# One subtile in two groups of four, in place of one in three, fetched row by row by the sync engine of a two-layer graph network

## What is computed

```python
h = relu(layernorm(x)); z = h @ W                       # per node
e = leaky_relu(el[src] + er[dst]); a = exp(e - emax[dst])
x = x + segment_sum(z[src] * a, dst) / segment_sum(a, dst) + bias
h = relu(layernorm(x)); s, v = h @ W_up                  # per node
w0..w3 = split(silu(silu(edge_f @ A1 + b1) @ A2 + b2) @ A3)
msg = [s[src]*y_s*w0, (v[src].y_v)*w3, s[src]*y_v*w1, v[src]*y_s*w2]
x = x + segment_sum(msg, dst) / 10 @ W_out
```

## Time and profile before

| | us |
|---|---|
| median of 3 runs (4036.51 to 4043.6) | 4041.5 |
| the profiled execution, its own time | 4049.47 |
| its span, first to last instruction | 4047.6 |
| POOL busy | 2961.1 (73%) |
| PE busy | 3048.9 (75%) |
| DVE busy | 1948.5 (48%) |
| ACT busy | 1119.0 (28%) |

### The profile page before, as it was taken

How to read it: one execution, slowest core, us unless ns; L and a number is a source line. 1 busy time by engine, 2 the same in 40 slices (tenths; PEclk the granted TensorE clock), 3 DMA queues, 4 the chain that set the end, 5 groups by cost and what they waited for, 6 DMA issues and landing times.

```text
span 4047.6 us, 71477 instructions
## 1 busy us (share of the span) xinstructions
PE 3048.9 (75%) x15640; PEld 2582.1 (64%) x15641; DVE 1948.5 (48%) x4563; ACT 1119.0 (28%) x1869; POOL 2961.1 (73%) x3121
## 2 busy tenths in 40 slices
PE   2566666666667656766659989888899898899898
PEld 2556665566667555665647767666677676676676
DVE  7434434333433433434345555555555555555554
ACT  2334434333433434333331111111111111111111
POOL 1777777777777777777747777777777777777775
PEclk9666666666655665666669888888988989988888
DMA  3434343443434343444422222222222222222221
GB/s 107 119 108 119 111 121 109 124 114 108 119 109 118 112 121 104 124 113 114 118 52 59 59 62 61 60 61 60 59 60 61 61 60 61 60 60 61 60 62 49
DMA packets 208656, 352.07 MB, mean 87 GB/s; under 512 B 99631, under 2 KB 129638, under 8 KB 208326
## 3 DMA queue, kind: packets, MB, share of 16 engines
q0 software_dynamic: 99328, 216.34, 21.3%
q1 hardware_dynamic: 108548, 130.56, 10.4%
q10 hardware_dynamic: 450, 2.44, 0.2%
HBM read 338.22 MB, written 10.85 MB: 86 GB/s over the span
## 4 chain that ended last, share of the span: by engine, by line
POOL 66%; issue 24%; DVE 2%; DMA 2%; PE 2%; POOLq 1%; DVEq 1%; SPq 1%; ACT 1%; ACTq 0%
POOL rows L534 66%; DMA rows<-z_tab,idx 1%; DMA rows<-up_tab,idx 1%; POOLq L280 1%; PE pair L1175 0%; SPq L333 0%; ACT L633 0%; POOLq L281 0%; DVE share L1036 0%; PE pair L1307 0%; DMA win_dram<-share 0%; DVE share L1128 0%; PE pair L1264 0%; DVEq L965 0%; PE pair L1270 0%
## 5 line engine op out<-in xcount | busy, mean ns | idle before, releaser
L534 POOL DMA_INDIRECT rows<-z_tab,idx x1552 | 1477.2, 952 | 554.6 <-issue 546.1
L534 POOL DMA_INDIRECT rows<-up_tab,idx x1552 | 1468.0, 946 | 510.3 <-issue 505.4
L1211 PE MATMUL pair<-acc 128*128 x3168 | 572.1, 327 | 443.3 <-ACT acc L621 441.0
L1211 PEld LDWEIGHTS pair<-acc 128*128 128x128 f32 x3168 | 555.3, 272 | 490.4 <-issue 490.4
L1307 PE MATMUL pair<-share 128*128 128x144 f32 x3136 | 833.8, 354 | 0.0
L1305 PEld LDWEIGHTS pair<-share 128*128 128x128 f32 x3136 | 577.1, 217 | 395.6 <-DVE share L1131 220.4
L1243 PE MATMUL pair<-share,acc 128*128 128x136 f32 x3136 | 676.6, 400 | 0.3
L1305 PE MATMUL pair<-share 128*128 128x48 f32 x3136 | 573.1, 268 | 101.3 <-DVE share L1131 101.1
L1243 PEld LDWEIGHTS pair<-share,acc 128*128 128x128 f32 x3136 | 639.2, 299 | 0.5 <-issue 0.4
L1128 DVE TENSOR_TENSOR share<-rows,pair 128x384 f32<-128x384 f32 x784 | 396.6, 547 | 412.7 <-DMA rows<-up_tab,idx 397.6
L1307 PEld LDWEIGHTS pair<-share 128*128 128x128 f32 x3136 | 544.7, 217 | 0.0
(11 more groups left out here) (172 smaller groups left out, 1890.2 us busy)
## 6 DMA issues: line engine op xcount, KB each, us to landing
acc<-dst_tab SPq DMA_DIRECT2D x198, 512.0 KB
lent<-z_tab SPq DMA_DIRECT2D x2060, 0.6 KB
lent<-up_tab SPq DMA_DIRECT2D x2060, 0.5 KB
rows<-z_tab,idx POOLq DMA_INDIRECT x1552
rows<-up_tab,idx POOLq DMA_INDIRECT x1552
ef_sb<-in_edge_f SPq DMA_DIRECT2D x198, 32.0 KB
z_tab<-rows SPq DMA_DIRECT2D x7, 504.0 KB, 3.2
y_sb<-in_edge_y SPq DMA_DIRECT2D x198, 16.0 KB
```

Source lines behind the costliest of these rows:

```text
L534: pool.indirect_dma_start(out=rows[:, s, t, 0:width], out_offset=None, in_=table, in_offset=bass.IndirectOffsetOnAxis(ap=indices[:, t:t + ...
L1211: mm = t.matmul(bank[6 + h][:, i * 16:i * 16 + 16], hotT[:, h, i * P:(i + 1) * P], er_flat[:, bass.ds(at, 1), :].rearrange("p a f -> p (a ...
```

## The change

`PER` becomes 2, so that a round is two groups; SP fetches one subtile in 64 in place of one in 96. `PARTS` becomes eight parts of 16 rows, in place of eight of 12 and four of 8. There are 24 rounds in a stage in place of 16, with one group left over in both. The table of the offsets (`lent_dram`) grows from 17 to 25 rows.

```diff
-PER = 3
+PER = 2
 LENT = GI // PER
-PARTS = (12,) * 8 + (8,) * 4
+PARTS = (16,) * 8
```

## The result

The kernel before took 4041.5 us (4036.51 to 4044.52, 5 runs), the changed one **4072.7 us** (4070.77 to 4090.51, 5 runs). The ratio is 1.0095, 95% interval 1.0068 to 1.0121: slower by about 31 us. The forecast was 4045 with a range of 4025 to 4080. The time lies in the range, but it is not "within 0.2%", which I had called likeliest.

The account below looks back on a forecast made before the run. The prediction took POOL's gathers to bound the kernel, with SP's store-to-store loop about as long in stage 1 after the change. Stage 1 +14 and stage 2 -10 gave +4 on 4041.5, so 4045 us, range 4025 to 4080.

Parts of the forecast that it names:

- within 0.2%: Whole kernel: time not told from no change, the forecast's own range of 4033 to 4050 us; chance 0.42.
- POOL as the bound, 1.251 us for each gather: Both stages: POOL waits for nobody, so each gather spared is worth 1.251 us while nothing else is as slow.
- Stage 2, -10: Stage 2: 8 gathers fewer save 10.0 us; SP's 389 us of added rows fit in its 610 us of waits.
- rival 4: Stage 2: SP fills up, at 0.6 us for a row in place of 0.38; above 4060 us, chance 0.03.
- The step with 16 rows: SP's plain step in stage 1 grows from 5.70 us with 12 rows to 7.22 with 16.
- Leg A: Stage 1, from one block's store to the next over a round's end: grows from 38.62 to 43.2 us.
- Leg B: Stage 1, store to next store inside a round: 36.2 us, with PE fast on the second of two tiles.
- rival 2: Stage 1: PE slow inside the round too, 3.5 us more in each of 18 legs, +63, about 4108; chance 0.09.
- A + B: Stage 1: both kinds of store-to-store leg together take 79.4 us, against 78.8 for POOL's 63 gathers.
- 18 us for 1 us: Stage 1: one microsecond more in the two legs' sum costs about 18 us, as 18 legs lie inside a round.
- rival 3: Stage 1: same loop, SP or landing slower, the two legs 79.7 to 81.5 us together; 4050 to 4080, chance 0.26.
- Rival 1: Stage 1: the store-to-store loop stays hidden behind POOL, its two legs under 78.8 us; 4022 to 4033, chance 0.20.

Follow-up runs that it names:

- f2: Changed kernel with the part of rows of tile 2 issued ahead of the block's store, not behind it; first chip: 4022.96 us, ratio 0.9951 to the kernel before.
- f4: Changed kernel with rounds of two groups in stage 1 only, stage 2 keeping three and parts of 12 and 8; first chip: 4094.9 us, ratio 1.0122.
- f1: The changed kernel run once more, nothing altered, beside the kernel before on the first chip: 4075.5 us, ratio 1.0086.
- e1: Changed kernel with the part of rows issued ahead of the wait for the finished block; second, slower chip: 5828 us, ratio 1.0161 to the kernel before.
- f3: Changed kernel with parts of (20, 12, 12, 20) rows twice in place of 16 each; first chip: 4236.3 us, ratio 1.0479 to the kernel before.

## Why the prediction was right or wrong, point by point

**POOL as the bound, 1.251 us for each gather: right.** f2, where nothing else binds, gives 20.4 us for 16 gathers.

**Stage 2, -10: right**, -11.3 in after and 10.0 between f4 and f1. SP's spare time was mis-sized. From 2140 to 4040 it waits:

```profile
SPq L281 <- ACT rows L627: 152.8, 24, 9.9
SPq L281 <- DVE share L1131: 1.7, 1, 1.7
```

Together 154.5 us in place of 610, where some 220 were foretold. So SP's waits shrank by 456 us rather than by 389; the eight round ends more are in that. It cost nothing, as 154 were still left. On the second chip this reserve is gone (in all of e1 SP waits 42 us for ACT's copy and 13 for DVE's products), and stage 2 loses: that is rival 4, which had 0.03. Its price of 0.6 us for a row is near the average there, but not because each added row costs that.

**The step with 16 rows: right.** 7.22 foretold, 7.23 measured.

**Leg A, 43.2: 0.55 short.** It is 43.74 on average in after and 43.79 in f1, of 19 legs; the targets leave at +18.7 in place of +18.2.

**Leg B, 36.2 always: this is the step that failed.** The average is 38.03 in after and 37.45 in f1. Most of the short ones are at 35.6 to 36.3 as worked out, but 7 to 10 of the 18 are 3.3 us longer. The prediction put it as "its work on tile 2's one-hot starts right behind that of the tile before, as at 1468.93", at 1.95 and 2.10. This row was no exception: of 25 such pairs between 180 and 2040 us of before (the first slow behind a pause, the second at most 1 us behind it), 19 are fast in the second tile. But it stood in another rhythm. Of before, the PE work on the tile ahead of that pair, which the earlier trace rows lacks:

```profile
1452.20 1.95 PE L1211 MATMUL pair<-acc 128*128 x16 [0.19 <-ACT acc L621]
```

From there to the slow start at 1461.42 are 9.2 us, and in all 19 fast cases of before it is 9.1 to 10.1. In the changed kernel this distance is 11.2 (1282.34 to 1293.50), where SP's steps are longer, and with 10.5 to 11.2 behind a fast tile 9 of 12 such pairs in f1 and 8 of 12 in after stay slow. The change had moved the distance at which the row stood. That this distance decides is not shown, and some rows speak against it: the six slow pairs of before have 9.4 to 10.3, and of the legs B of f3 four with 12.3 or 12.4 behind a fast tile, at pauses of 7.3 to 8.4, are fast in the second tile, while eight with 12.0 to 12.5 are slow. What is shown is that the second tile has two lengths and that the leg follows it. I had this as rival 2, but as all or nothing: always slow, 4108, chance 0.09. Half of it came.

**The sum.** A + B is 81.8 in after and 81.2 in f1, against 79.4. By "18 us for 1 us" this is +43 and +32, of which leg A's 0.55 makes 10 and leg B's 1.8 and 1.25 make 33 and 22. Stage 2 starts 51.0 and 40.9 us later than before, in place of 14: +37 and +27. The rule held roughly and its input didn't. By place: group 37's first store comes at 1651.76 in after and 1645.20 in f1, against 1609.04, so the lag is 43 and 36 us there, where I put 4. I had counted it from group 20 on; 26 and 21 us of it stood already at group 20's store (960.12 and 954.96, against 934.44). From group 37's store to that of group 48 (2101.68 and 2091.63, against 2043.29) it grows by 16 and 12, where the double blocks and the groups without one were to give 10. A term that I hadn't at all is the last leg: from group 48's first store to the next are 23.16 us in after and f1, and were 30.55 before, so 7 us of the lag are won back there.

```profile
1651.76 8.76 SPq L407 DMA_DIRECT2D up_tab<-acc  x2
...
2101.68 0.36 SPq L407 DMA_DIRECT2D up_tab<-acc  x1
```

So the elaborate count at the end of stage 1 was good to a few us, and the stretch before it held the loss: with A + B at 79.4 the loop keeps pace with POOL's 78.8, with 81.5 each round loses 2.7.

**The rivals.** The time is rival 3's (4050 to 4080), but its cause makes only a quarter to a third of the excess: leg A's 0.55, of which 0.5 is SP's. The rest is rival 2's cause in half of the legs. That the stated range held the time is partly luck, as its upper end came from rival 3 and not from a mixture of fast and slow legs. Rival 1, the loop hidden, needed A + B under 78.8. It fell here; f2 makes it come true by a shorter loop.

**The chances.** "Within 0.2%" had 0.42 and needed both legs right to 1 us in 79. With a bimodal PE in the loop, whose two levels stood in the rows, the mean of the two lengths (37.9, so A + B = 81.1, and 18 x 1.7 = +31, near 4075) had to be a case of its own.

## What to carry to other kernels

Count the work that stands between a wait and the next link of a closed loop: the same part of 16 rows costs 52 us over the launch behind the store and nothing ahead of it (f1 against f2), in a queue that waits there anyway. When an engine's speed depends on its own rhythm, a row gives its speed only for the rhythm in which it stood; look at what the change does to the distance ahead of it, and price both levels. Where a change turns spare issue time of a queue into a gain, ask how much of it is left on a chip on which that queue is slower: f2 is 0.5% faster on one chip and e1, the same code, 1.6% slower on the other.

## What the runs showed of the hardware

- Two chips ran the same kernel in 4043 and in 5758 to 5853 us. The medians of single instructions are the same (a gather 944 ns, SP's transfer issue 228, its MOVE 29); on the slower chip SP's instructions stall now and then, up to 1.4 us each, so that a row of stage 1 costs 0.59 us on average in e1 in place of 0.33 in f2. Where the stalls come from is open.
- TensorE's line L1211 goes back and forth between 3.59 and 1.95 us within one loop of fixed program, at a granted clock of 0.60 on average. Each leg in which it is slow on the second tile makes the launch 3.4 to 3.8 us longer. The runs of one kernel probably differ by it: 4070.8 to 4090.5 for after, 4022.2 to 4024.1 for f2, where POOL is the bound.
